# First attention: row maxima by single 512-wide matmuls between the score matmuls, one maximum of two keys by ScalarE's relu of their difference, and denominators inverted in a 128 x 8 tile by way of DRAM

## The reference, cut to what matters

```python
x = x + _L0_xattn_ref(_layernorm(x), ctx_1024, Wq, Wk, Wv, Wo, bo)   # the stage of this change
# seven more layers follow, which the change leaves as they are

q, k, v = split_heads(x @ Wq), split_heads(context @ Wk), split_heads(context @ Wv)  # 8 heads of 64
sim = jnp.einsum('bhid,bhjd->bhij', q, k) * 64 ** -0.5     # 2048 queries, 1601 keys
attn = jax.nn.softmax(sim, axis=-1)
out = jnp.einsum('bhij,bhjd->bhid', attn, v)
return out @ Wo + bo
```

## Time and profile before

| | |
|---|---|
| median of 3 executions | 2823.01 us (2810.94 to 2833.49) |
| profiled execution, its own time | 2821.8 us |
| span of the profiled execution | 2820.0 us |
| busy: TensorE, weight loads | 2473.9 us (88%), 1269.9 us (45%) |
| busy: VectorE | 1821.0 us (65%) |
| busy: ScalarE, GpSimd | 1196.4 us (42%), 509.5 us (18%) |
| granted TensorE clock, mean | 0.915 |
| first attention: first maxima, first score, last attend | at 50.0, 72.2, 740.4 us |

### The profile page before, as it was taken

How to read it: one execution, slowest core, us unless ns; L and a number is a source line. 1 busy time by engine, 2 the same in 40 slices (tenths; PEclk the granted TensorE clock), 3 DMA queues, 4 the chain that set the end, 5 groups by cost and what they waited for, 6 DMA issues and landing times.

```text
span 2820.0 us, 32986 instructions
## 1 busy us (share of the span) xinstructions
PE 2473.9 (88%) x12476; PEld 1269.9 (45%) x12476; DVE 1821.0 (65%) x3631; ACT 1196.4 (42%) x1580; POOL 509.5 (18%) x281
## 2 busy tenths in 40 slices
PE   8999999998767884999897999885999999999878
PEld 3322222223322233778664677663444444443377
DVE  5676777887568766233453244483786888887386
ACT  2343433434345431122441223450365666666753
POOL 0333333333222226200002540000000000000011
PEclk8999999999869997999997999885697999999989
...
DMA packets 47866, 93.49 MB, mean 33 GB/s; under 512 B 7211, under 2 KB 32441, under 8 KB 46681
## 3 DMA queue, kind: packets, MB, share of 16 engines
...
## 4 chain that ended last, share of the span: by engine, by line
PE 55%; DVE 13%; ACT 3%; issue 2%; DMA 2%; ACTq 0%; SPq 0%; POOL 0%; DVEq 0%; POOLq 0%
PE PS L2374 7%; PE PS L1297 6%; PE PS L2355 5%; DVE pm L2479 4%; PE PS L2317 4%; PE PS L914 4%; PE PS L1255 2%; PE PS L1278 2%; PE PS L1280 2%; PE PS L1279 2%; PE PS L896 1%; PE PS L2398 1%; PE PS L373 1%; DVE xg L324 1%; PE PS L1072 1%
## 5 line engine op out<-in xcount | busy, mean ns | idle before, releaser
L2479 DVE TENSOR_REDUCE pm<-PS 128x1 f32<-128x512 f32 x768 | 479.3, 684 | 100.5 <-PE PS L2317 100.4
L2445 ACT ACTIVATE P<-PS 128x1024 f32<-128x1024 f32 (+1 forms) x416 | 407.7, 1021 | 213.8 <-PE PS L2355 212.2
L2317 PE MATMUL PS<-Ks,Qs 49*128 49x512 f32 x768 | 314.8, 491 | 41.3 <-DMA Qs<-row 26.5
L682 ACT ACTIVATE P<-PS 128x1024 f32<-128x1024 f32 (+1 forms) x208 | 212.7, 1024 | 319.3 <-PE PS L597 296.5
L714 DVE TENSOR_REDUCE pm<-PS 128x1 f32<-128x400 f32 (+1 forms) x512 | 265.2, 563 | 74.6 <-PE PS L563 72.2
L2355 PE MATMUL PS<-Qs,Ks 51*128 51x512 f32 (+1 forms) x832 | 281.0, 451 | 8.6 <-ACT P L2445 8.6
L2374 PE MATMUL PS<-P,V 128*17 128x512 f32 (+1 forms) x1664 | 231.7, 630 | 0.3 <-ACT P L2445 0.3
L610 PE MATMUL PS<-P,V 128*64 128x512 f32 (+1 forms) x832 | 227.2, 625 | 4.9 <-ACT P L682 4.9
L2355 PEld LDWEIGHTS PS<-Qs,Ks 51*128 51x128 f32 (+1 forms) x832 | 140.5, 191 | 191.3 <-ACT P L2445 148.6
L520 POOL TENSOR_TENSOR odd<-odd,P 128x1024 f32<-128x1024 f32 x64 | 164.6, 2572 | 257.3 <-ACT P L682 257.3
L2317 PEld LDWEIGHTS PS<-Ks,Qs 49*128 49x128 f32 x768 | 136.3, 198 | 138.3 <-DVE pm L2479 91.1
...
## 6 DMA issues: line engine op xcount, KB each, us to landing
...
Qs<-q_parts SPq DMA_DIRECT2D x90, 64.0 KB, 2.4
...
```

Of the source, the lines that this page charges most:

```text
L682: e.activation(self.P[0:r, n % 4, :, :], PS[0:r, b:b + 2, :], ACT.Exp, scale=0.125).then_inc(*k.ac_exp.up(("A", n)))
L2317: m = e.matmul(PS[:, b, :], self.Qs[rows, s, pr, q0:q0 + 128], self.Ks[rows, s, pr, cs], start=True, stop=not masked)
L2445: e.activation(self.P[0:r, n % 4, :, :], PS[0:r, b:b + 2, :], ACT.Exp, scale=0.25).then_inc(*k.ac_exp.up((3, n)))
L2479: e.tensor_reduce(self.pm[:, u % 2, i, c:c + 1], PS[:, ring.of(("max", key)), :], AX.X, ALU.max).then_inc(*k.dv_max.up((3, *key)))
```

## The change

- "max" is now a step of one matmul of 512 columns on one row half. For each query tile and half there are three kinds. "over" multiplies with the difference of keys 0 to 511 and keys 512 to 1023 (new tile `Kd`, made by VectorE once for each pair of heads), and ScalarE takes its relu into a tile `over`. "base" multiplies with keys 512 to 1023, and VectorE adds `over` and takes the maximum in one instruction (`tensor_tensor_reduce`, compiled to two, the second reads the accumulator), which is the maximum over both halves of these 1024 keys. "last" is keys 1024 to 1535 with a reduction as before. A step "rest" takes the last 66 keys of all four query tiles into one bank, with one reduction of 264 columns for four results.
- The maxima stand between the two row halves of score matmuls: one after the first matmul with the high keys, one after the first with the low queries, 26 for each unit, and eight of them ahead of the first score. The score step is cut into its eight matmuls for this.
- The denominators: SyncE copies one row of `R` for each half into `Rc`, 128 partitions x 8, VectorE inverts this tile, SyncE writes it to DRAM, waits, and reads it back on 64 partitions for each half. The reciprocal stands directly behind "den" in the list, "norm" four places later.
- The projections for the next pair stand in two units of a pair instead of three, four in each. The places among the key tiles are 25 instead of 50.

```diff
@@ -394,6 +396,9 @@
         self.Ql = scope.place("Ql", [128, 2, N], BF16)
         self.Kh = scope.place("Kh", [128, 2, M], BF16)
         self.Kl = scope.place("Kl", [128, 2, M], BF16)
+        self.Kd = scope.place("Kd", [128, 2, 512], BF16)
+        self.over = scope.place("over0", [128, 3, 512], F32)
+        self.trash = scope.place("trash0", [128, 2, 512], BF16)
...
-        self.pm = scope.place("pm0", [128, 2, 32], F32)
+        self.Rc = scope.place("Rc0", [128, 8], F32)
+        self.pm = scope.place("pm0", [128, 2, 8, 3], F32)
...
     def max_steps(self, u):
-
-        steps = [[(self, "max", (x, qt, c)) for qt in range(4) for c in range(4)] for x in (u, u + 1)]
-        return (steps[0][3 if u else 0:] + [(self, "rows", (u,))] + [None] * 2 + [(self, "turn", (u,))]
-                + (steps[1][:3] if u < 15 else []))
+        return [(self, "max", (u, qt, kind, hh)) for qt in range(4) for kind in ("over", "last", "base")
+                for hh in (1, 0)] + [(self, "rest", (u, hh)) for hh in (1, 0)]
+
+    def rows_steps(self, u):
+        return [(self, "rows", (u,)), None, (self, "turn", (u,))]
 
     def divide_steps(self, u):
-        return [(self, "den", (u,))] + [(self, "recip", (u, i)) for i in range(4)] + [(self, "norm", (u,))]
+        return [(self, "den", (u,)), (self, "recip", (u,))] + [None] * 4 + [(self, "norm", (u,))]
...
-        out += self.qk_steps(0) + self.max_steps(0)
+        ahead = 8
+        maxima = [s for u in range(16) for s in self.max_steps(u)]
+        out += self.qk_steps(0) + maxima[:26] + self.rows_steps(0) + maxima[26:26 + ahead]
+        done = 26 + ahead
         before = None
+        later = []
         for u in range(16):
             p, qb = u // 4, u % 4
             parts = []
             if u:
-                parts += [(self.divide_steps(u - 1), 0.07, 0.36), (self.project_steps(u - 1), 0.4, 0.65)]
-            if p < 3 and qb < 3:
-                parts.append((self.qk_steps(p + 1)[3 * qb:3 * qb + 3], 0.0, 0.9))
-            if u < 15:
-                parts.append((self.max_steps(u + 1), 0.0, 0.98))
-            slots = spread(weave(*parts), 50)
+                parts += [(self.divide_steps(u - 1), 0.07, 0.5), (self.project_steps(u - 1), 0.52, 0.78)]
+            if p < 3 and qb < 2:
+                parts.append((self.qk_steps(p + 1)[4 * qb:4 * qb + 4], 0.0, 0.9))
+            slots = spread(weave(*parts), 25)
             for kt in range(KT):
-                out.append((self, "score", (u, kt, 0)))
-                out += slots[4 * kt - 2] if kt else []
-                out.append((self, "score", (u, kt, 1)))
-                out += slots[4 * kt - 1] if kt else []
+                for part in ("Kh", "Kl", "Ql", "mr"):
+                    out.append((self, "score", (u, kt, part, 0)))
+                    if part in ("Kh", "Ql") and done < len(maxima):
+                        out.append(maxima[done])
+                        if maxima[done][1] == "rest" and maxima[done][2][1] == 0:
+                            later = self.rows_steps(maxima[done][2][0])
+                        done += 1
+                    out.append((self, "score", (u, kt, part, 1)))
+                    if part == "Kl" and kt:
+                        out += slots[2 * kt - 1]
                 if before:
                     out.append((self, "attend", before))
                     if before[1] == KT - 1:
                         out += [(self, "take", before[:1]), (self, "sum", before[:1])]
                 before = (u, kt)
-                out += slots[4 * kt]
-                out += slots[4 * kt + 1]
+                out += later[:1] + slots[2 * kt]
+                later = later[1:]
...
+        elif step == "recip":
+            u, = key
+            at.wait_ge(k.ac_misc, ("R", u))
+            for hh in range(2):
+                e.dma_start(self.Rc[64 * hh:64 * hh + 64, :], self.R[64 * hh:64 * hh + 1, :]).then_inc(
+                    *self.ld_den.up((u, hh), 16))
+            at.wait_ge(k.dv_misc, ("recip", u))
+            e.dma_start(self.dd.rearrange("h (p n) -> (h p) n", n=8), self.Rc[:]).then_inc(*self.st_den.up(u, 16))
+            at.wait_ge(self.st_den, u)
+            for hh in range(2):
+                e.dma_start(self.R[64 * hh:64 * hh + 64, :], self.dd[hh:hh + 1, :].to_broadcast([64, 512])).then_inc(
+                    *self.ld_rec.up((u, hh), 16))
...
@@ -552,16 +585,28 @@
                              stop=hf == 1)
             m.then_inc(*k.pe_proj.up(("A", *key)))
         elif step == "max":
-            u, qt, c = key
+            u, qt, kind, hh = key
             p, s = u // 4, u // 4 % 2
             q0 = u % 4 * 512 + qt * 128
-            k0, kn = CHUNKS[c]
-            for hh in range(2):
-                rows = slice(64 * hh, 64 * hh + 64)
-                b = ring.take(at, ("max", key, hh))
+            rows = slice(64 * hh, 64 * hh + 64)
+            b = ring.take(at, ("max", key))
+            if kind == "over":
+                keys = self.Kd[rows, s, :]
+                at.wait_ge(k.dv_proj, ("A", p, "difference"))
+            else:
+                keys = self.Kh[rows, s, (512, 1024)[kind == "last"]:(1024, 1536)[kind == "last"]]
                 at.wait_ge(k.ac_proj, ("A", p, "k", 3))
-                m = e.matmul(PS[:, b, 0:kn], self.Qh[rows, s, q0:q0 + 128], self.Kh[rows, s, k0:k0 + kn], start=True,
-                             stop=True)
+            e.matmul(PS[:, b, :], self.Qh[rows, s, q0:q0 + 128], keys, start=True, stop=True).then_inc(
+                *k.pe_max.up(("A", *key)))
+        elif step == "rest":
+            u, hh = key
+            s = u // 4 % 2
+            rows = slice(64 * hh, 64 * hh + 64)
+            b = ring.take(at, ("rest", key))
+            for qt in range(4):
+                q0 = u % 4 * 512 + qt * 128
+                m = e.matmul(PS[:, b, 66 * qt:66 * qt + 66], self.Qh[rows, s, q0:q0 + 128],
+                             self.Kh[rows, s, M - 66:M], start=True, stop=True)
...
-            if part == 0:
+            rows, ps = slice(64 * hh, 64 * hh + 64), PS[0:r, 2 * (n % 2) + hh, :]
+            if part == "Kh":
                 if n >= 2:
                     at.wait_ge(k.ac_exp, ("A", n - 2))
                 at.wait_ge(k.dv_proj, ("A", u // 4, "k", 3))
-                for kk, start in ((self.Kh, True), (self.Kl, False)):
-                    for hh in range(2):
-                        rows = slice(64 * hh, 64 * hh + 64)
-                        e.matmul(PS[0:r, b + hh, :], kk[rows, s, ks], self.Qh[rows, s, q], start=start, stop=False)
+                e.matmul(ps, self.Kh[rows, s, ks], self.Qh[rows, s, q], start=True, stop=False)
+            elif part == "Kl":
+                e.matmul(ps, self.Kl[rows, s, ks], self.Qh[rows, s, q], start=False, stop=False)
+            elif part == "Ql":
+                e.matmul(ps, self.Kh[rows, s, ks], self.Ql[rows, s, q], start=False, stop=False)
             else:
                 at.wait_ge(k.ac_rows, ("A", u))
-                for hh in range(2):
-                    rows = slice(64 * hh, 64 * hh + 64)
-                    e.matmul(PS[0:r, b + hh, :], self.Kh[rows, s, ks], self.Ql[rows, s, q], start=False, stop=False)
-                for hh in range(2):
-                    rows = slice(64 * hh, 64 * hh + 64)
-                    m = e.matmul(PS[0:r, b + hh, :], k.onesb[rows, 0:r], self.mr[rows, u % 2, :], start=False,
-                                 stop=True)
-                m.then_inc(*k.pe_score.up(("A", n)))
+                m = e.matmul(ps, k.onesb[rows, 0:r], self.mr[rows, u % 2, :], start=False, stop=True)
+                if hh:
+                    m.then_inc(*k.pe_score.up(("A", n)))
...
-        elif step == "score" and key[2] == 1:
-            u, kt, _ = key
+        elif step == "max" and key[2] == "over":
+            u, qt, _, hh = key
+            n = 8 * u + 2 * qt + 1 - hh
+            at.wait_ge(k.pe_max, ("A", *key))
+            if n > 2:
+                v, i = (n - 3) // 8, (n - 3) % 8
+                at.wait_ge(k.dv_max, ("A", v, i // 2, "base", 1 - i % 2))
+            e.activation(self.over[:, n % 3, :], PS[:, ring.of(("max", key)), :], ACT.Relu).then_inc(
+                *self.ac_over.up(key))
+            ring.freed["max", key] = (self.ac_over, key)
...
+            if kind == "k" and c == 2:
+                if p > 1:
+                    at.wait_ge(k.pe_max, ("A", 4 * (p - 2) + 3, 3, "base", 0))
+                s = p % 2
+                e.tensor_tensor(self.Kd[:, s, :], self.Kh[:, s, 0:512], self.Kh[:, s, 512:1024],
+                                ALU.subtract).then_inc(*k.dv_proj.up(("A", p, "difference")))
+        elif step == "max" and key[2] != "over":
+            u, qt, kind, hh = key
+            n = 8 * u + 2 * qt + 1 - hh
+            i = 4 * hh + qt
             at.wait_ge(k.pe_max, ("A", *key))
-            for hh in range(2):
-                i = 16 * hh + 4 * qt + c
```

(31 more changed lines are left out.)

17 lines of the change are left out of this document (10 added, 7 removed).

## The result

The changed kernel takes 2814.07 us (median of 20 runs, 2800.13 to 2838.15) against 2827.24 for the kernel before (20 runs, 2810.94 to 2839.81). The ratio is 0.9958, 95% interval 0.9941 to 0.9975: faster by 7 to 17 us, where 43 were forecast. 2814 lies 4 us above the upper end of the range.

What follows compares the result with a forecast made beforehand. TensorE and VectorE, each near full, coupled by three PSUM banks and fixed orders, bind it. Floor 568, stalls 29, half clock 12, other waits 12: 621 for 665, -44; start -3, tail +4, total -43: 2780 us, range 2750 to 2810.

Steps and rivals of the forecast that it cites:

- neighbours on different halves overlap: TensorE's score and maxima matmuls: any two neighbours on different row halves pair at 0.22 us, a two-maxima tile takes 2.18.
- the rule on weight loads: TensorE tiles: weight loads overlap only across row groups, so same-half successions cost 39 us, result 2819; chance 0.03.
- The floor: TensorE's summed matmul times over the attention phase without waits: 570 us before, 568 after the change.
- the relu's possible cost in late exponentials: ScalarE in tiles with two relus: exponentials up to 0.5 us later, priced at 0, bound 13 us.
- a sign of being wrong: DMAs of the reciprocals: a landing row above 2.4 us would make the prediction wrong.
- rival 5: Clock and order waits nearly vanish: 605 us, -60, giving 2762, or 2752 with better bounds at start and tail; chance 0.15.
- stalls at the denominators 29, half clock 12, and 12 for bank and order waits: The units' sum: these three terms on TensorE's floor of 568 give 621 us in place of 665, -44.
- the norm's and the additions' durations stay: VectorE in the units: norm and additions were taken to last as long as before the change.
- the 65 to 70 us that I put down to reductions: Part of TensorE's 95 us excess before the change said to hang on VectorE's reductions; most was to go.
- The tail: From the denominators' copy to wo after the last unit: 7.9 us in place of 4.3, +4, bounds +2 to +8.
- rival 1: Gain under 28 us (2796 to 2820): denominator stalls keep the clock falling, slowed additions hold banks; chance 0.13.
- The argument against it, unit 15 before: Against rival 1: the last unit, without maxima, loses nothing; it took 30.0 us where the terms give 30.3.

Runs made afterwards that it cites:

- the busy wait: Changed kernel plus 13 or 5 matmuls doing no kernel work ahead of TensorE's wait for GpSimd's sum; ratio 0.9926 to the kernel before, phase 630.0 us.

## Why the prediction was wrong

**What held.** That neighbours on different halves overlap (2.19 against 2.18); the durations of base, last, rest, relu and the small reciprocal; the reductions' waits nearly gone; the start (-2.9 against -3; over all profiles the first key tile came at 71.8 to 74.4 us with the new start and at 75.7 to 76.5 with the old); the sign. The 39 us by the rule on weight loads did not show: a tile with two maxima takes 2.19 us. The floor came out at 564, forecast 568. Of the relu's possible cost in late exponentials (0, bound 13) nothing shows: the three waits for exponentials, 5.9 us, have another cause, below.

**What held in part.** The first two landings were priced right, but the last, priced at 2.2 us, took 2.9 in the median, above the 2.4 that the prediction names as a sign of being wrong. The norm waited for it only in the tail. The 2.0 us that the prediction cites from the Trainium skill ("DMA: Bandwidth & Descriptors", anatomy of one DMA) stand there for DMAs issued from GpSimd, and these are SyncE's; their medians here are 1.8, 1.4 and 2.9. Unit 11 took 33.4 us, forecast 35, but units 4 and 8 took 52.5 and 48.2, where 41 to 44 were forecast. Two figures of the prediction don't follow from its terms: rival 5's 568 + 29 + 5 + 3 gives 2764, and 2759 with the better bounds, not 2762 and 2752; and of the 512 reductions removed, the 32 of unit 0 stand ahead of the phase.

**The step that failed** is the sum's line of what stays, "stalls at the denominators 29, half clock 12, and 12 for bank and order waits". It gives 53 us, and 80 were there:
- The stalls: 31 us. This was sized right, in each unit within 0.7 us (1.1 to 3.4 us, forecast 1.2 to 2.7).
- Half clock: 13 to 14 by the busy wait, at most 19 by the granted 0.97. Forecast 12.
- Order waits: what is left, 80 - 31 - 14 = 35, forecast 12. This term is the miss. I read it as the remainder of the waits for reductions, with VectorE's slowed additions, and took the other orders at nothing. With the denominators later the stall and its half clock are gone, and 603 - 564 = 39 us stay (2.6 of them a new wait for the norm in unit 15), so the term is no part of them. The tiles show 8.5 us for projections and wo steps that stand between two groups of score matmuls, 0.2 to 0.35 each (8 went when they stood between tiles); 6.7 for wo behind the norm; 5.9 for exponentials in the last pair's units; 2.3 for reductions. The remaining 12 are spread over many tiles, and no run isolates them.

The prediction said "the norm's and the additions' durations stay". The norm went from 0.99 to 2.25 us, 2.84 where wo waits for it, because in its new place one of GpSimd's additions runs beside it. One place earlier it took 0.69 and the phase, with the denominators later, lost 11 us. The Trainium skill ("SBUF — State Buffer", two separate sides) says that GpSimd and a VectorE operation with two inputs in SBUF exclude each other. The trace agrees: the norm of 2.85 us starts at 308.13, within GpSimd's addition from 307.77 to 310.44. I weighed that for "base" and left it out for the norm, to which it applies.

In the last pair each unit's norm takes a Sqrt from ScalarE, in the middle of the exponentials. Around it, in unit 13, the profile after has:

```profile
620.38 1.28 ACT L352 ACT_TABLE_LOAD   x1
...
621.69 0.21 ACT L352 ACTIVATE rstd<-rstd 128x4 f32<-128x4 f32 x1
621.80 0.58 ACT L717 ACTIVATE over<-PS 128x512 f32<-128x512 f32 x1
...
622.39 1.28 ACT L733 ACT_TABLE_LOAD   x1
...
623.69 1.94 ACT L733 ACTIVATE P<-PS 128x1024 f32<-128x1024 f32 x2
624.77 1.63 PE L651 MATMUL PS<-P,V 128*64 128x512 f32 x4 [1.99 <-ACT P L733]
```

Two table loads of 1.28 us make the attend matmuls 2 us late, three times, with half clock behind it. The kernel before has this too:

```profile
PE PS L610 <- ACT P L682: 4.9, 3, 2.7
```

It lies inside the 65 to 70 us that I put down to reductions; so part of what the change was to win was never theirs.

**The tail** was +6.2 in place of +4, from the last key tile: 0.3 ahead of the denominators' copy, the chain itself 8.3 - 4.3 = 4.0 longer, and the other 1.9 in steps that the change leaves alone, at a granted clock of 0.66 from wo to the gate rows, before 0.71. With -2.9 at the start, -20.0 in the units and +6.2 the profile gives -16.7 at the gate rows, and whole runs say -7 to -17.

**The sizes of the rivals.** The time fell into rival 1 (gain under 28 us, 2796 to 2820), which had 0.13. Of its terms the order waits of 30 us came true (35), though not by "slowed additions"; the half clock of 30 did not (14), and the exponentials' 13 did not either. The argument against it, unit 15 before, said nothing about a unit with a stall in it.

**What the profile could have told.** The 29 us stood in my own sum as a cost of the order, and moving the denominators shows that 41 hung on them; by the busy wait a third of that is the clock that falls with the stall. They also hid the rest: with the stall in place the way by DRAM costs 4 us and the new maxima give 8; without it they give 26 and 42.
